# A scan layer on one Trainium2 core: the work that prepares the next block is put at other steps

## The chip, the core and the metric

The kernel runs on one core of one Trainium2 chip. The metric is the device time of one execution in microseconds (us), lower is better. Before the change it is 2182.27 us, the median of 3 runs (2181.54 to 2183.92). One more execution was recorded by the profiler: its own time is 2181.55 us, and its span, from the first to the last instruction, 2179.8 us.

## The reference

The program is a decoder of six stages. Only the first is touched, a selective state-space (Mamba) layer over 2 sequences of 1024 rows with 256 features. `hidden_states` is the normalised input; its result is added to the input.

```python
D_MODEL, D_STATE, D_CONV = 256, 16, 4
D_INNER, DT_RANK = 512, 16
x, z = split(hidden_states @ in_proj_w.T)
x = silu(causal_conv(x, conv_w, 4 taps) + conv_b)
A = -exp(A_log)
dt, Bm, C = split(x @ x_proj_w.T)              # 16, 16, 16 columns
dt = softplus(dt @ dt_proj_w.T + dt_proj_b)
def step(h, ins):                              # over the 1024 rows
    h = exp(dt_t[:, :, None] * A) * h + dt_t[:, :, None] * B_t[:, None, :] * x_t[:, :, None]
    y = einsum('bdn,bn->bd', h, C_t)
y = ys + x * D
return y * silu(z) @ out_proj_w.T
```

## The kernel before

The 2048 rows are cut into NK = 4 **blocks** of W = 512 rows; blocks 1 and 2 are the first sequence, 3 and 4 the second (the code counts them k = 0 to 3). The 512 inner channels are CI = 4 groups of 128, and there are NS = 16 states. A block is NU = 64 **steps** p = 0 to 63, one for each state and channel group: step p has state p // 4 and group p % 4, on a tile of 128 channels by 512 rows. One step passes through all engines:

- ScalarE multiplies dt·x by B in a layout with the rows in partitions, one quarter of a state's tile per step (`times_b`, into `UT`), and makes the decay exp(dt·A) (`decay`, into `dA`).
- TensorE turns the product into the layout with channels in partitions (`bring_u`, into one of two PSUM banks).
- VectorE runs the recurrence over 512 rows in one instruction (`scan`, into a ring `H` of 8 tiles).
- GpSimd multiplies two steps' states by C in one instruction, after the even and the odd step are both scanned (`times_c`, into a ring `HC` of 8).
- TensorE turns `HC` back and sums it over the states in PSUM banks 0 to 3 (`sum_up`), LAG = 5 steps later.

Each engine takes its instructions strictly in the order of the program, and engines wait on each other by semaphores. `bring_u` of step G waits until scan G-2 has ended; `decay` of step G until scan G-6 has; the first `times_b` of a state until the `bring_u` of the state before it has ended; `sum_up` until `times_c` has. So the order in which each engine's list is written out decides what a wait holds up.

Besides the 64 steps each block carries the **preparation** of the block after it and the end of the block before it, written out by tables of step numbers in the five engines' loops. On the preparation's path lie: the projection of x (`project_x`), the convolution of 4 instructions for each group on VectorE (`convolve`), silu (`silu_x`), the projections to B, C and dt (`project_rows`, `transpose_b`, `project_dt`), softplus in pieces on ScalarE, VectorE and GpSimd (`magnitude`, `rectify`, `correct`, `logarithm`, `add_logarithm`), the product with x (`times_x`) and its transpose (`transpose_dtx`, `keep_dtx`). The end of a block is the gate with silu(z) on VectorE (`gate`), transposes of the gated tile (`transpose_gated`, `keep_gated`), the output projection (`project_out`) and the addition to the rows (`add_rows`). Silu and logarithm each need another function table on ScalarE than exp, so that a table load stands before and after them.

PSUM banks 6 and 7 are shared by all of the preparation; `bank(i, ...)` makes TensorE wait until the last user of the bank has been read.

Of the kernel before, what the change touches and what calls it, by code (L numbers as in the profile page):

```python
# [6 lines left out]
ALU = mybir.AluOpType  # L7
# [7 lines left out]
P = 128  # L15
# [208 lines left out]
G_ORDER = (0, 2, 1, 3)  # L224


def mamba(g, a):
    nc = g.nc
    PS = g.PS
    with ExitStack() as ctx:  # L230
# [53 lines left out]
        with nc.Block() as block:  # L284
# [24 lines left out]
            def _(pe):  # L309
# [64 lines left out]
                def transpose_dtx(k, c):  # L374

                    out = bank(c % 2, dtxt_ready, k * CI + c + 1)
# [12 lines left out]
                def transpose_gated(k, i):  # L389

                    t = G_ORDER[i]
                    out = bank(t % 2, g_ready, k * TC + i + 1)
# [5 lines left out]
                def project_out(k, t, half):  # L398

                    if half == 0:  # L400
                        if t % 2 == 0:
                            held[t // 2] = bank(t // 2, o_used, k * 2 + t // 2 + 1)
                        pe.wait_ge(g_ready, (k + 1) * TC)
                    out = held[t // 2][:, t % 2 * D:(t % 2 + 1) * D]
# [16 lines left out]
                def sum_up(G):  # L421
# [3 lines left out]
                    if u == 0 and k:  # L425
                        pe.wait_ge(y_used, k * TC)
                    pe.wait_ge(hc_ready, G + 1)
                    for t in range(TC):
                        ins = pe.matmul(PS[t][:, c * P:(c + 1) * P], HC[:, G % YR, t * P:(t + 1) * P], g.ident[:, :],  # L429
                                        start=(u == 0), stop=(u == NU - 1), is_transpose=True, skip_group_check=True)  # L430
# [17 lines left out]
                for k in range(NK):  # L448
                    for p in range(NU):
# [3 lines left out]
                        if 8 <= p < 11:  # L453
                            sum_up(k * NU + 2 * (p - 8))
                            sum_up(k * NU + 2 * (p - 8) + 1)
                        elif p >= 11:
                            sum_up(k * NU + p - LAG)
                        if k + 1 < NK:
# [4 lines left out]
                            if p in (10, 11, 14, 15):  # L463
                                project_x(k + 1, 2 + (p - 10) // 4, p % 2)
                        if k and p in (8, 9, 12, 13):
                            transpose_gated(k - 1, (8, 9, 12, 13).index(p))
                        if p in (12, 13, 18, 19):
                            if p == 12 and k == 0:
                                pe.wait_ge(diag_ready, 1)
                            add_skip(k, (12, 13, 18, 19).index(p))  # L470
                        if p in (16, 17, 20, 21):
                            project_z(k, (p - 16) // 4, p % 2)
                        if k + 1 < NK:
                            if 23 <= p < 27:
                                project_rows(k + 1, p - 23)
                            if p == 27:
                                transpose_b(k + 1)
                            if 28 <= p < 32:
                                project_dt(k + 1, p - 28)
                        if k and 32 <= p < 40:  # L480
                            project_out(k - 1, (p - 32) // 2, p % 2)
                        if 40 <= p < 44:
                            project_z(k, 2 + (p - 40) // 2, p % 2)
                        if k + 1 < NK and p in (46, 50, 54, 58):
                            transpose_dtx(k + 1, (p - 46) // 4)
# [9 lines left out]
            def _(act):  # L495
# [53 lines left out]
                def keep_dtx(k, c):  # L549

                    act.wait_ge(dtxt_full, k * CI + c + 1)
                    act.activation(DTXT[:, k % 2, :, c * P:(c + 1) * P], PS[6 + c % 2][:, :].rearrange("p (t n) -> p t n", t=TC),
                                   ACT.Copy).then_inc(dtxt_ready, 1)

                def keep_gated(k, i):

                    t = G_ORDER[i]
                    act.wait_ge(g_full, k * TC + i + 1)
# [49 lines left out]
                for k in range(NK):  # L608
                    for p in range(NU):
# [6 lines left out]
                        if k and p in (9, 10, 13, 14):  # L616
                            keep_gated(k - 1, (9, 10, 13, 14).index(p))
                        if p == 20:
# [2149 lines left out]
```

## Time and profile before

| what | value |
|---|---|
| median of 3 runs | 2182.27 us (2181.54 to 2183.92) |
| the profiled execution: time, span | 2181.55 us, 2179.8 us |
| first scan starts, last scan ends | 57.0 us, 613.9 us |
| block 1, 2, 3, 4, first scan to the next block's first scan (block 4: to its last scan's end) | 151.0, 152.1, 152.8, 101.1 us |
| busy from 57 to 614 us: PE, DVE, ACT, POOL | 421.1, 368.7, 396.7, 380.3 us of 557 |
| mean granted TensorE clock from 57 to 614 us | 0.87 |

The scan layer is the first 634 us of the span; the five stages behind it are the same code in both kernels. No engine is busy for more than four fifths of the layer. Block 4 has no next block to prepare and takes 50 us less than each of the others.

### The profile page before, as it was taken

How to read it: one execution, taken by the hardware profiler on the slowest of the kernel's cores; microseconds unless marked ns; L12 is line 12 of the kernel's file. 1: busy time of each engine (PE TensorE's matmuls, PEld its weight loads, DVE VectorE, ACT ScalarE, POOL GpSimd, SP SyncE). 2: the span in 40 equal slices, each digit the busy share in tenths (PEclk: the TensorE clock that was granted, in tenths of full speed). 3: DMA queues.
4: the chain of work that ended last, by engine and by line, in shares of the span. 5: the costliest groups of instructions: out<-in, count | busy, mean ns of one | idle time of the engine just before them, and what ended most of it. 6: DMA issues, size and time to landing. Idle time of an engine off the chain costs nothing. (4 is left out here: it accounts for less than half of the span.)

```text
span 2179.8 us, 28324 instructions
## 1 busy us (share of the span) xinstructions
PE 1572.5 (72%) x9844; PEld 1325.8 (61%) x9844; DVE 1119.2 (51%) x2193; ACT 912.1 (42%) x1599; POOL 930.2 (43%) x615
## 2 busy tenths in 40 slices
PE   4776866857868974863038996898692199989990
PEld 1555655657656863861027895895592088878880
DVE  6755756746767951225766345645847023222322
ACT  4775776767834442532124223744331022322220
POOL 0577576577643334651023112402005723685406
PEclk7988988988979976985558998899895599999995
DMA  3001010101011032520010001002005311333103
GB/s 110 20 21 39 20 40 20 40 20 40 20 63 28 1 117 98 187 75 23 0 47 1 1 1 42 1 11 69 1 1 210 104 63 49 126 114 109 30 20 118
DMA packets 51958, 114.44 MB, mean 53 GB/s; under 512 B 13996, under 2 KB 34377, under 8 KB 44276
## 3 DMA queue, kind: packets, MB, share of 16 engines
q1 hardware_dynamic: 43764, 75.23, 10.0%
q0 software_dynamic: 8064, 37.45, 5.1%
q8 instruction: 85, 1.39, 0.3%
q14 instruction: 45, 0.37, 0.1%
HBM read 87.02 MB, written 25.87 MB: 52 GB/s over the span
## 5 line engine op out<-in xcount | busy, mean ns | idle before, releaser
L839 POOL TENSOR_TENSOR HC<-H,CB 128x1024 f32<-128x1024 f32 x128 | 302.5, 2364 | 165.7 <-DVE H L739 103.7
L418 PE MATMUL ps<-ident,UT 128*128 128x128 f32 x1024 | 182.1, 307 | 58.5 <-DVE H L739 52.4
L739 DVE TENSOR_TENSOR_SCAN H<-dA,ps 128x512 f32<-128x512 f32 x128 | 154.0, 1214 | 124.6 <-PE ps L418 86.2
L418 PEld LDWEIGHTS ps<-ident,UT 128*128 128x128 f32 x1024 | 136.7, 158 | 131.0 <-DVE H L739 72.0
L570 ACT ACTIVATE UT<-DTXT,BT 128x512 f32<-128x512 f32 x256 | 181.4, 711 | 39.3 <-PE ps L418 39.2
L739 DVE TENSOR_TENSOR_SCAN H<-dA,HL,ps 128x512 f32<-128x512 f32 x128 | 160.2, 1275 | 71.7 <-PE ps L418 46.0
L580 ACT ACTIVATE dA<-DT,nA 128x512 f32<-128x512 f32 x256 | 180.8, 709 | 2.8 <-DVE DT L707 2.7
L429 PE MATMUL ps<-ident,HC 128*128 128x128 f32 x1024 | 171.5, 298 | 9.7 <-POOL HC L839 9.2
L1748 POOL TENSOR_TENSOR f_W<-f_stage,f_zeros 128x2048 fp32r<-128x2048 f32 x24 | 86.5, 3606 | 144.6 <-POOLq L1768 138.6
L429 PEld LDWEIGHTS ps<-ident,HC 128*128 128x128 f32 x1024 | 138.1, 157 | 12.5 <-POOL HC L839 10.9
L1965 DVE TENSOR_TENSOR f_XN<-f_XN,ps 128x1024 f32<-128x1024 f32 x39 | 47.6, 1221 | 173.5 <-PE ps L147 173.5
L145 PE MATMUL ps<-f_W,f_DIT 128*128 x312 | 128.7, 412 | 8.8 <-POOL f_W L1750 7.1
L146 PE MATMUL ps<-f_W,f_DIT 128*128 x312 | 125.0, 401 | 0.0
L147 PE MATMUL ps<-f_W,f_DIT 128*128 x312 | 124.9, 400 | 0.0
L1750 POOL TENSOR_TENSOR f_W<-f_stage,f_W 128x2048 fp32r<-128x2048 f32 x24 | 110.3, 4595 | 1.9
L1958 DVE TENSOR_TENSOR f_HT<-ps,f_HT 128x512 fp32r<-128x512 f32 x78 | 50.2, 686 | 100.9 <-ACT f_HT L1862 100.9
L1519 POOL TENSOR_TENSOR f_l<-f_w,f_h 128x2048 fp32r<-128x2048 f32 x16 | 73.5, 4596 | 64.2 <-ACT f_h L1580 63.5
L138 PE MATMUL ps<-ident,h_XN 128*128 128x128 f32 x96 | 29.4, 432 | 84.7 <-DVE h_XN L96 59.3
L1873 ACT ACTIVATE f_EO<-ps 128x256 f32<-128x256 f32 x39 | 14.9, 383 | 179.6 <-PE ps L147 179.6
L145 PE MATMUL ps<-f_W,f_HT 128*128 x312 | 87.8, 281 | 1.8 <-issue 1.8
L146 PE MATMUL ps<-f_W,f_HT 128*128 x312 | 87.9, 282 | 0.0
L147 PE MATMUL ps<-f_W,f_HT 128*128 x312 | 87.8, 282 | 0.0
(490 smaller groups left out, 4306.7 us busy)
## 6 DMA issues: line engine op xcount, KB each, us to landing
f_stage<-in_f_w POOLq DMA_DIRECT2D x24, 1024.0 KB, 5.4
CB<-m_c_rows SPq DMA_DIRECT2D x16, 1024.0 KB, 4.7
f_w<-in_f_w SPq DMA_DIRECT2D x16, 1024.0 KB
f_rows_in<-f_zeros SPq DMA_DIRECT2D x13, 384.0 KB, 13.6
f_DI<-f_rows_in SPq DMA_DIRECT2D x39, 128.0 KB, 2.2
f_rows_out<-f_EO SPq DMA_DIRECT2D x39, 128.0 KB, 1.7
a_values<-a_zeros SPq DMA_DIRECT2D x8, 320.0 KB, 5.4
a_VBD<-a_values SPq DMA_DIRECT2D x8, 320.0 KB, 4.5
```

The costliest lines, as they stand in the source:

```text
L145: pe.matmul(out, ah, bh, start=first, stop=False)
L146: pe.matmul(out, ah, bl, start=False, stop=False)
L147: return pe.matmul(out, al, bh, start=False, stop=last)
L418: ins = pe.transpose(PS[4 + G % UR][:, t * P:(t + 1) * P], UT[:, n % 2, t, c * P:(c + 1) * P], g.ident[:, :])
L429: ins = pe.matmul(PS[t][:, c * P:(c + 1) * P], HC[:, G % YR, t * P:(t + 1) * P], g.ident[:, :], start=(u == 0), stop=(u == NU - 1), is_tra ...
L570: act.activation(UT[:, N % 2, t, :], DTXT[:, k % 2, t, :], ACT.Copy, scale=BT[:, k % 2, t, n:n + 1]).then_inc(ut_ready, 1)
L580: act.activation(dA[:, G % AR, :], DT[:, k % 2, c, :], ACT.Exp, scale=nA[:, c, n:n + 1]).then_inc(da_ready, 1)
L739: dve.tensor_tensor_scan(H[:, G % HR, :], dA[:, G % AR, :], PS[4 + G % UR][:, :], first, ALU.mult, ALU.add).then_inc(h_ready, 1)
L839: pool.tensor_tensor(HC[:, y:y + 2, :], H[:, s:s + 2, :], CB[:, n // 4 % CR, n % 4:n % 4 + 1, :].to_broadcast([P, 2, W]), ALU.mult).then_i ...
L1519: pool.tensor_tensor(l[:, e % 2, :, :], w[:, e % WR, :, :], h[:, e % 2, :, :].bitcast(F32), ALU.subtract).then_inc(wl_ready, 1)
L1748: pool.tensor_tensor(hi, stage[:, q, :], zeros[:, 0:1].to_broadcast([P, PART]), ALU.add).then_inc(hi_ready, 1)
L1750: pool.tensor_tensor(lo, stage[:, q, :], hi.bitcast(F32), ALU.subtract).then_inc(lo_ready, 1)
```

## The change

It keeps every computation of the layer and moves the preparation to other steps, in the lists of all five engines. The new positions (before in brackets): x projection of groups 2 and 3 at steps 7, 8, 10, 11 (10, 11, 14, 15); two convolution instructions a step at steps 4, 5, 7, 8, 9, 10, 12, 13 (one a step at 4 to 19); silu of x after step 14 (20); projections to B, C and dt at steps 15 to 24 (23 to 31); magnitude and rectify at 21, 22, 24, 25 (29 to 32); correct at 24, 27, 30, 33 (30, 32, 34, 36); the logarithms after step 37, behind the first two silus of z (40, and silus of z at 20); add_logarithm at 39, 43, 47, 51 (42, 46, 50, 54) and times_x at 41, 45, 49, 53 (44, 48, 52, 56) on GpSimd; transpose_dtx at 47, 51, 55, 59 (46, 50, 54, 58) on TensorE. The z projections stand at 32 to 35 and 38 to 41 (16, 17, 20, 21 and 40 to 43), the gated transposes at 26, 27, 29, 30 (8, 9, 12, 13) and the output projection at 44 to 54 (32 to 39), with add_rows at 48 and 55 (36 and 40).

Three things are more than a new place. The product with D, which was added into the sums at steps 12 to 19, now opens them at steps 6 to 9 (`begin_sums`) and waits there for the gate of the same rows; the sums over states start at step 10 instead of 8, three at step 10 and two at 11 to 13. All four transposes of dt·x use bank 6 alone, where they alternated between two. The output projection uses bank 7 alone. The product with C is over two steps in both kernels; only a loop over single steps is put around it, so that other work can stand behind an odd step.

```diff
-                    out = bank(c % 2, dtxt_ready, k * CI + c + 1)
+                    out = bank(0, dtxt_ready, k * CI + c + 1)
...
-                def add_skip(k, t):
-
+                def begin_sums(k, t):
+
+                    if k:
+                        pe.wait_ge(y_used, (k - 1) * TC + t + 1)
                     for c in range(CI):
                         ins = pe.matmul(PS[t][:, c * P:(c + 1) * P], XS[:, c, t * P:(t + 1) * P], skip_diag[:, c, :],
-                                        start=False, stop=False, skip_group_check=True)
+                                        start=(c == 0), stop=False, skip_group_check=True)
...
-                            held[t // 2] = bank(t // 2, o_used, k * 2 + t // 2 + 1)
+                            held[1] = bank(1, o_used, k * 2 + t // 2 + 1)
...
-                        if 8 <= p < 11:
-                            sum_up(k * NU + 2 * (p - 8))
-                            sum_up(k * NU + 2 * (p - 8) + 1)
-                        elif p >= 11:
+                        if p == 10:
+                            sum_up(k * NU)
+                        if 10 <= p < 14:
+                            sum_up(k * NU + 2 * p - 19)
+                            sum_up(k * NU + 2 * p - 18)
+                        elif p >= 14:
                             sum_up(k * NU + p - LAG)
...
-                        if k + 1 < NK and p in (46, 50, 54, 58):
-                            transpose_dtx(k + 1, (p - 46) // 4)
+                        if k + 1 < NK and p in (47, 51, 55, 59):
+                            transpose_dtx(k + 1, (p - 47) // 4)
...
-                            if 42 <= p < 58 and p % 4 == 2:
-                                add_logarithm(k + 1, (p - 42) // 4)
-                            if 44 <= p < 60 and p % 4 == 0:
-                                times_x(k + 1, (p - 44) // 4)
+                            if p in (39, 43, 47, 51):
+                                add_logarithm(k + 1, (p - 39) // 4)
+                            if p in (41, 45, 49, 53):
+                                times_x(k + 1, (p - 41) // 4)
```

TensorE in block 2, before, around the first transpose of dt·x (L379 of `DTX`, step 46); L418 is bring_u, L429 sum_up, L347 the z projection of step 43:

```order
L347 MATMUL ps<-w_in,XT 128x512
L418 MATMUL ps<-ident,UT 128x128 x4
L429 MATMUL ps<-ident,HC 128x128 x4
L418 MATMUL ps<-ident,UT 128x128 x4
L429 MATMUL ps<-ident,HC 128x128 x4
L418 MATMUL ps<-ident,UT 128x128 x4
L429 MATMUL ps<-ident,HC 128x128 x4
L379 MATMUL ps<-ident,DTX 128x128 x4
```

The same place in the changed kernel (step 47; bring_u is L418, sum_up L427, the output projection L406, the transpose L378):

```order
L406 MATMUL ps<-m_w_out,GD 128x256 x2
L418 MATMUL ps<-ident,UT 128x128 x4
L427 MATMUL ps<-ident,HC 128x128 x4
L406 MATMUL ps<-m_w_out,GD 128x256 x2
L418 MATMUL ps<-ident,UT 128x128 x4
L427 MATMUL ps<-ident,HC 128x128 x4
L378 MATMUL ps<-ident,DTX 128x128 x4
L418 MATMUL ps<-ident,UT 128x128 x4
L427 MATMUL ps<-ident,HC 128x128 x4
L406 MATMUL ps<-m_w_out,GD 128x256 x2
```

The transpose stands one step later, and the output projection is now among these steps. The sum_up in front of it is that of step 41 before and of step 42 now.

ScalarE in block 2, before, behind step 40: the logarithms (L547), then times_b (L570) and decay (L580) of step 41:

```order
L547 ACT_TABLE_LOAD
L547 ACTIVATE EA<-EA 128x512 x4
L570 ACTIVATE UT<-DTXT,BT 128x512
L580 ACT_TABLE_LOAD
L580 ACTIVATE dA<-DT,nA 128x512
```

And in the changed kernel, behind step 37 (silu of z L523, logarithm L550, times_b L572, decay L582):

```order
L523 ACT_TABLE_LOAD
L523 ACTIVATE ZT<-ps 128x512 x2
L550 ACT_TABLE_LOAD
L550 ACTIVATE EA<-EA 128x512 x4
L572 ACTIVATE UT<-DTXT,BT 128x512
L582 ACT_TABLE_LOAD
L582 ACTIVATE dA<-DT,nA 128x512
```

The first two silus of z, which stood behind silu_x at step 20, are now in front of the logarithms, with a table load of their own.

GpSimd in block 2, before, at the corrections (L808 to L810, three instructions for a channel group); L839 is times_c:

```order
L839 TENSOR_TENSOR HC<-H,CB 128x1024 x17
L808 TENSOR_SCALAR DTX<-EA 128x512
L809 TENSOR_SCALAR DTX<-DTX 128x512
L810 TENSOR_TENSOR DTX<-EA,DTX 128x512
L839 TENSOR_TENSOR HC<-H,CB 128x1024
```

And in the changed kernel, from the corrections of the first group (L812 to L814) to times_c and the second group's:

```order
L843 TENSOR_TENSOR HC<-H,CB 128x1024 x14
L812 TENSOR_SCALAR DTX<-EA 128x512
L813 TENSOR_SCALAR DTX<-DTX 128x512
L814 TENSOR_TENSOR DTX<-EA,DTX 128x512
L843 TENSOR_TENSOR HC<-H,CB 128x1024
```

The first count includes the last product of block 1, so that 16 products of block 2 stood ahead of the first correction and 13 stand there now.

## Rows read from the trace of the kernel before

**Rows 1.** Busy time by block (stretch, then PE, PEld, DVE, ACT, POOL, clock, DMA).
```profile
57.00:208.00 151.00, 107.71 (x610) 82.78 (x609) 92.93 (x90) 101.88 (x160) 101.08 (x76) 0.84 0.06 22
208.00:360.00 152.00, 113.85 (x669) 89.69 (x668) 98.85 (x99) 105.63 (x167) 100.29 (x58) 0.87 0.08 29
360.00:513.00 153.00, 113.56 (x666) 89.83 (x666) 94.50 (x93) 104.15 (x164) 103.19 (x77) 0.85 0.07 28
513.00:614.00 101.00, 85.94 (x604) 72.73 (x602) 82.44 (x70) 84.99 (x134) 75.73 (x34) 0.95 0.09 32
```

**Rows 2.** Who waited for whom, blocks 2 and 3 (us in total, times, longest).
```profile
DVE H L739 <- PE ps L418: 76.2, 52, 7.0
...
PE ps L379 <- POOL DTX L824: 45.9, 8, 6.3
...
DVE H L739 <- ACT dA L580: 33.1, 12, 7.2
```

**Rows 3.** Busy time, block 2: steps 0 to 20, and steps 41 to 58.
```profile
208.00:248.50 40.50, 36.84 (x236) 28.91 (x235) 38.68 (x46) 28.55 (x46) 25.42 (x12) 0.92 0.15 53
...
298.30:348.00 49.70, 26.64 (x142) 24.18 (x142) 22.45 (x18) 27.80 (x43) 35.36 (x21) 0.73 0.06 21
```

**Rows 4.** GpSimd in order of time, block 2 (start, duration, instruction, idle before it).
```profile
315.93 2.37 POOL L839 TENSOR_TENSOR HC<-H,CB 128x1024 f32<-128x1024 f32 x1 [3.63 <-issue]
318.25 1.29 POOL L818 TENSOR_TENSOR DTX<-DTX,EA 128x512 f32<-128x512 f32 x1
...
320.84 2.34 POOL L839 TENSOR_TENSOR HC<-H,CB 128x1024 f32<-128x1024 f32 x1
323.13 1.26 POOL L824 TENSOR_TENSOR DTX<-DT,XS 128x512 f32<-128x512 f32 x1
328.03 2.38 POOL L839 TENSOR_TENSOR HC<-H,CB 128x1024 f32<-128x1024 f32 x1 [3.63 <-issue]
```

**Rows 5.** TensorE in order of time, block 2, the second transpose of dt·x.
```profile
324.54 1.08 PE L379 MATMUL ps<-ident,DTX 128*128 128x128 f32 x4 [5.30 <-POOL DTX L824]
```

**Rows 6.** VectorE in order of time, block 2: steps 26 and 27, 31 and 32, 51.
```profile
263.49 1.28 DVE L739 TENSOR_TENSOR_SCAN H<-dA,HL,ps 128x512 f32<-128x512 f32 x1 [0.73 <-PE ps L418]
265.51 1.28 DVE L739 TENSOR_TENSOR_SCAN H<-dA,HL,ps 128x512 f32<-128x512 f32 x1 [0.73 <-PE ps L418]
...
273.32 1.28 DVE L739 TENSOR_TENSOR_SCAN H<-dA,HL,ps 128x512 f32<-128x512 f32 x1 [0.43 <-ACT dA L580]
...
275.69 1.28 DVE L739 TENSOR_TENSOR_SCAN H<-dA,HL,ps 128x512 f32<-128x512 f32 x1 [0.50 <-ACT dA L580]
...
326.61 1.28 DVE L739 TENSOR_TENSOR_SCAN H<-dA,HL,ps 128x512 f32<-128x512 f32 x1 [6.24 <-PE ps L418]
```

**Rows 7.** GpSimd, block 2: the products on either side of one correction.
```profile
279.73 2.38 POOL L839 TENSOR_TENSOR HC<-H,CB 128x1024 f32<-128x1024 f32 x1
...
284.72 2.38 POOL L839 TENSOR_TENSOR HC<-H,CB 128x1024 f32<-128x1024 f32 x1
```

**Rows 8.** ScalarE, block 2: the silus behind step 20.
```profile
246.43 1.28 ACT L515 ACT_TABLE_LOAD   x1
247.72 2.19 ACT L515 ACTIVATE XS<-DT 128x512 f32<-128x512 f32 x4
249.82 1.09 ACT L520 ACTIVATE ZT<-ps 128x512 f32<-128x512 f32 x2
```

**Rows 9.** ScalarE, block 2: the last logarithm, behind step 40.
```profile
294.78 0.63 ACT L547 ACTIVATE EA<-EA 128x512 f32<-128x512 f32 x1 [3.18 <-POOL DTX L810]
```

**Rows 10.** VectorE, block 2: steps 60 and 61, and the first scan of block 3.
```profile
352.43 1.28 DVE L739 TENSOR_TENSOR_SCAN H<-dA,HL,ps 128x512 f32<-128x512 f32 x1 [0.35 <-PE ps L418]
353.62 1.12 DVE L663 TENSOR_SCALAR m_XN<-X,m_mv,m_rstd 128x256 f32<-128x256 f32 x1
354.67 1.27 DVE L739 TENSOR_TENSOR_SCAN H<-dA,HL,ps 128x512 f32<-128x512 f32 x1
...
360.03 1.21 DVE L739 TENSOR_TENSOR_SCAN H<-dA,ps 128x512 f32<-128x512 f32 x1
```

More of the change, by code:

```diff
@@ L429, in sum_up @@
                         ins = pe.matmul(PS[t][:, c * P:(c + 1) * P], HC[:, G % YR, t * P:(t + 1) * P], g.ident[:, :],
[L430 removed]
+                                        start=False, stop=(u == NU - 1), is_transpose=True, skip_group_check=True)
                     ins.then_inc(hc_used, 1)
@@ L462, in _ @@
                                 project_x(k + 1, (p - 2) // 2, p % 2)
[L463 to L468, printed above, removed]
+                            if p in (7, 8):
+                                project_x(k + 1, 2, p - 7)
@@ L477, in _ @@
                                 transpose_b(k + 1)
[L478 to L483, printed above, removed]
-                        if k + 1 < NK and p in (46, 50, 54, 58):
-                            transpose_dtx(k + 1, (p - 46) // 4)
+                            if p in (20, 21, 23, 24):
+                                project_dt(k + 1, (20, 21, 23, 24).index(p))
@@ new lines, in _ @@
+                        if k and p in (26, 27, 29, 30):
+                            transpose_gated(k - 1, (26, 27, 29, 30).index(p))
+                        if 32 <= p < 36:
+                            project_z(k, (p - 32) // 2, p % 2)
+                        if 38 <= p < 42:
+                            project_z(k, 2 + (p - 38) // 2, p % 2)
+                        if k + 1 < NK and p in (47, 51, 55, 59):
+                            transpose_dtx(k + 1, (p - 47) // 4)
+                        if k and p in (44, 45, 46, 48, 50, 52, 53, 54):
+                            i = (44, 45, 46, 48, 50, 52, 53, 54).index(p)
+                            project_out(k - 1, i // 2, i % 2)
@@ L721, in add_rows @@
                     rows = g.X[:, k * TC + 2 * j:k * TC + 2 * j + 2, :]
-                    dve.tensor_tensor(rows, rows, PS[6 + j][:, :].rearrange("p (t d) -> p t d", t=2), ALU.add).then_inc(o_used, 1)
+                    dve.tensor_tensor(rows, rows, PS[7][:, :].rearrange("p (t d) -> p t d", t=2), ALU.add).then_inc(o_used, 1)
                 def scan(G):
@@ L848, in _ @@
                 for k in range(NK):
-                    for p in range(0, NU, 2):
-                        times_c(k * NU + p)
+                    for p in range(NU):
+                        if p % 2 == 0:
+                            times_c(k * NU + p)
                         if k + 1 < NK:
-                            if p == 2 and (k + 1) % KB:
+                            if p == 3 and (k + 1) % KB:
                                 edges(k + 1)
-                            if 30 <= p < 38:
-                                correct(k + 1, (p - 30) // 2)
-                            if 42 <= p < 58 and p % 4 == 2:
-                                add_logarithm(k + 1, (p - 42) // 4)
-                            if 44 <= p < 60 and p % 4 == 0:
-                                times_x(k + 1, (p - 44) // 4)
+                            if p in (24, 27, 30, 33):
+                                correct(k + 1, (p - 24) // 3)
+                            if p in (39, 43, 47, 51):
+                                add_logarithm(k + 1, (p - 39) // 4)
+                            if p in (41, 45, 49, 53):
+                                times_x(k + 1, (p - 41) // 4)
 NH, HD, SK = 16, 16, 77
```

83 lines of the change are left out of this document (41 added, 42 removed).

## The prediction

> **What bounds the kernel now.** I read the busy time by block first. Blocks 1 to 3 take 151, 152 and 153 us for 64 steps, block 4 takes 101, and no engine fills any of them: the fullest, ScalarE, is busy 105.63 of 152 us in block 2, GpSimd 100.29 and VectorE 98.85 [rows 1]. So the layer is bound by waits in blocks 1 to 3, and their shortest possible length is set by the fullest engine, not by 152. The rest of the program, from 634 us on, is untouched by the change.
>
> The view of who waited for whom says which waits. In blocks 2 and 3 the scan waited 76.2 us for TensorE and 33.1 us for the decay [rows 2]. TensorE was no bound itself: it waited 45.9 us, eight times, in front of the transpose of dt·x for GpSimd's product with x [rows 2], and bring_u stood behind it. The order of time shows one such turn. From GpSimd's times_c at 315.93 to the next turn's at 328.03 are 12.10 us, of which it works without a gap from 315.93 to 323.13 + 1.26 = 324.39, that is 8.46 us, and then idles 3.63 us [rows 4]. TensorE starts its transpose at 324.54, as soon as the product is there, after 5.30 us idle [rows 5], and the scan that comes behind it starts at 326.61 after 6.24 us idle [rows 6]. It is a closed chain: scan, times_c, times_x, transpose, bring_u, scan. Between steps 41 and 58 GpSimd is busy 35.36 of 49.7 us and TensorE, at a mean clock of 0.73, 26.64 [rows 3].
>
> The scan's waits for the decay are table loads on ScalarE: behind step 20 a load of 1.28 us and six silus of 2.19 + 1.09 us [rows 8], behind step 40 four logarithms, of which the last waited 3.18 us for GpSimd's correction [rows 9].
>
> **The change at the transposes (steps 38 to 59).** The two kernels' lists on GpSimd are alike here, three steps earlier, and TensorE's transposes stand one step later. The lead grows from 2 steps to 6. More than that, the wait can't come back: at step 47 + 4c TensorE first does the sum of step 42 + 4c, which needs times_c of that pair, and GpSimd has times_x(c) in front of that times_c. Whoever waits for the sum has waited for the product with x already. What is late next is GpSimd's own work, 8.46 us for four steps against 12.10.
>
> **GpSimd as the bound (steps 24 to 55).** The corrections move from steps 30 to 36 up to 24 to 33, and add_logarithm to 39. So from times_c of step 24 to that of step 54 GpSimd holds 16 products with C and all of its extra work. Four turns at 8.46 us hold eight of the products; four products with a correction take 284.72 - 279.73 = 4.99 us each [rows 7]; four more are bare at 2.37 us [rows 4]. Sum: 33.8 + 20.0 + 9.5 = 63.3 us. The scan alone would need about 1.2 us a step (354.67 less the 1.12 us of L663 less 352.43, and the mutual overlap of some 0.1) [rows 10], 37 us for 31 steps; ScalarE and TensorE have less extra work there than GpSimd. A lag of some five steps is allowed (the sum of step p - 5 stands behind bring_u of step p), which the end of this stretch uses up.
>
> The logarithms, behind step 37, do cost a wait for the decay: three loads of 1.28, two silus of 1.09, four logarithms of some 0.6 each, then an ordinary step of 1.2, in all 8.6 us, against two scans that are still supplied (2.4): some 6 us without a scan. By my reckoning GpSimd works through them, since it then stands behind by two plain products and two with a correction (2 x 2.37 + 2 x 4.99 = 14.7 us), so that they add nothing. If it had no such lag they would add the 6 us; this is the second rival. The last logarithm finds its correction ready, three steps of distance in place of four but without the extra products behind it.
>
> Behind the stretch: the sum and the last transpose, 0.5 and 0.9 us, the copy 0.6, and one ScalarE step of 1.2 until scan 60, because the first times_b of the new block needs all four transposed groups; then steps 60 to 63 as before, 360.03 - 352.43 = 7.6 us [rows 10]. Sum 10.8.
>
> **The front of the block.** Steps 0 to 13 now hold what VectorE had in 0 to 19: all sixteen convolution instructions and the gates. In the old stretch of 21 scans it was busy 38.68 of 40.5 us [rows 3]; seven scans fewer are 38.68 - 8.4 = 30.3 busy, and with the same small gaps 31.7 us. TensorE has room: it was busy 36.84 us at a clock of 0.92 for 21 steps, and the z projections and gated transposes leave. The opening of the sums waits for gates that VectorE does at steps 5 and 6, a step before TensorE needs them; I take nothing for it (0 to 1.5 us a block).
>
> Step 14: the last silu can start only when step 13's convolution ends. Then 0.55 (a quarter of 2.19) + 1.28 for the load back + 1.2 for the ordinary pair = 3.0 us until the next scan. In blocks 1 and 3 all four silus wait for the edge of the convolution: 1.6 more. Steps 15 to 23 carry the projections to B, C and dt as 23 to 31 did: between 2.02 us (265.51 - 263.49) and 2.37 us (275.69 - 273.32) where there is a projection [rows 6], less at the two steps without; 9 x 2.0 = 18.0 us. Steps 24 and 25, until GpSimd starts the long stretch: 3.6.
>
> **Sum for block 2:** 31.7 + 3.0 + 18.0 + 3.6 + 63.3 + 10.8 = 130.4 us against 152: 21.6 less. Blocks 1 and 3 move the same work, with 1.6 us more at step 14 and somewhat less elsewhere (no gates in block 1, no normalisation at the end of block 3): 21 each. Block 4 has no preparation; its silus, z and output projections are only placed elsewhere: 0 (bounds -5 and +3, the waits at its two table episodes). At the end of the layer the second half of the output projection waits for add_rows in bank 7, about +1 us, and the gated transposes no longer share a bank two by two, about -1. In all -63 to -64.
>
> The places at which no row can show a wait (triple sums at step 10, the gates, four copies of dt·x through a single bank, ScalarE reaching step 59 before TensorE) I put at 1.2 us a block, bounds 0 and 6 us. That makes **-60 us**: 2181.55 - 60 = 2121.6 for the profiled execution, whose own time is 0.7 us under the median, so 2122.
>
> **A rule on table loads.** Each of blocks 1 to 3 has seven loads instead of six. The rows: the load at 246.43 takes 1.28 us, and the silu starts at 247.72, right behind it [rows 8]. The Trainium skill (ScalarE: Activation LUTs, section What ACT_TABLE_LOAD costs) gives about 1.28 us for the load and about 1.38 us for a drain with it, 2.66 us for every switch. By that rule the three added loads would be an estimated 8 us of ScalarE's time instead of 3.8. The trace has no such drain between the two rows, so the sum stays with 1.28.
>
> **Rivals.**
> 1. *GpSimd isn't behind when ScalarE loads tables.* Then the 6 us behind step 37 stand in the sum by themselves, and only what the transposes and the front give is left: 3 x 6 = 18 us back, 2140. For it: at step 40 before, the scan was held by the same kind of work. Against it: GpSimd has 20 us of corrections and products in ten steps there. Chance 0.22.
> 2. *VectorE's normalisation waits for GpSimd.* At step 60 it takes 1.12 us for 256 columns [rows 10], more than half a scan. If GpSimd never rests at a block's end, all four in blocks 1 and 2 meet a product in flight, with up to 2.37 us and 1.2 in the mean to wait; a little over 3 us more for each of the two blocks, 2128. The Trainium skill (SBUF — State Buffer, section SBUF: two separate sides) says that GpSimd and such a VectorE operation take a shared port exclusively, for a whole instruction. Chance 0.08.
> 3. *The waits go and the time stays,* because ScalarE or TensorE take GpSimd's place for the whole of it. Against it: ScalarE is busy 105.63 of 152 us, TensorE 113.85 [rows 1]; either would have to keep 40 us of idle time. Chance 0.03, 2180.
> 4. *Slower: TensorE at its lower level where its work is crowded.* Steps 0 to 23 now hold the x projections, the opening of the sums, triple sums and all the projections to B, C and dt in a row. If the 1.2 GHz level held there, the 26 us of work that I count in steps 0 to 13 (36.84 less the work of seven plain steps and the projections that leave) would be 52 against 31.7, and steps 15 to 23 would take 35 instead of 18: +37 a block, +111 in all against the 60 saved. It decides from a little over half of these steps at the lower level; at three quarters the time is 2205. Against it: the granted clock was 0.92 in the old front [rows 3] and 0.95 in block 4, the block with the fewest idle times [rows 1]; it was low, 0.73, where TensorE waited. Chance 0.05.
>
> **Numbers.** The forecast, 2122, has 0.62. A measurement of this kernel can tell 0.2%, some 4 us, from no change. Faster by more than that are the forecast and rivals 1 and 2: 0.92; within 0.2% 0.03, slower 0.05. Range: from 2102 (no hidden waits, -5 in block 4, and the projection steps nearer to 1.5 us) to 2150 (rival 1 with 3 us a block of hidden waits).
>
> **What would show it.** Right: the waits of the transpose (L378) for times_x near nothing; blocks 1 to 3 at 128 to 134 us; GpSimd busy for over nine tenths from times_c 24 to 54, through the episode behind step 37; a mean clock of TensorE above 0.87; block 4 within 5 us of 101. Wrong: a GpSimd idle time of 5 us behind step 37 (rival 1), normalisations of 2 us (rival 2), ScalarE waiting at the copies of dt·x, or steps 0 to 13 longer than 36 us.

## The result, and the profile after

The changed kernel takes 2118.54 us, the median of 4 runs (2118.11 to 2121.53), against 2183.1 us, the median of 4 runs of the kernel before taken with it. The ratio is 0.9705, 95% interval 0.9688 to 0.9722: 3.0% faster, 64.6 us. The forecast was 2122.

Busy time by block in the changed kernel (columns as in [rows 1]; the blocks begin at their first scans at 59.6, 194.1, 325.9 and 458.6 us):

```profile
59.60:194.00 134.40, 104.03 (x609) 77.54 (x607) 92.79 (x89) 102.17 (x161) 100.62 (x76) 0.88 0.07 24
194.10:326.00 131.90, 105.24 (x670) 80.10 (x670) 99.02 (x100) 105.99 (x168) 100.25 (x58) 0.96 0.09 33
326.00:458.50 132.50, 103.62 (x664) 77.04 (x662) 94.44 (x92) 103.68 (x165) 102.84 (x76) 0.97 0.09 33
458.50:552.30 93.80, 82.68 (x605) 68.54 (x604) 82.04 (x71) 84.72 (x134) 75.80 (x34) 1.00 0.10 35
```

The four blocks are 134.5, 131.8, 132.6 and 93.7 us long, against 151.0, 152.1, 152.8 and 101.1 [rows 1]: 16.5, 20.3, 20.2 and 7.4 less. The work of VectorE, ScalarE and GpSimd in them is the same to 1 us; what went is idle time. TensorE has the same matmuls and is busy 9 and 10 us less in blocks 2 and 3, at a mean granted clock of 0.96 and 0.97 against 0.87 and 0.85. The first scan starts 2.7 us later than before, and what stands behind the last scan takes 1.7 us less. Together -63.3 us of span.

The transpose of dt·x waited 45.9 us for GpSimd in blocks 2 and 3 [rows 2]. In all of the trace its waits for GpSimd are gone; what is left is this (the view of the line L378, the former L379):

```profile
its engine sat idle before it (us, times) until:
  ACT DTXT L555: 17.4, 6
  issue: 7.5, 1
  DVE DTX L711: 6.0, 1
```

TensorE still waits for GpSimd in these two blocks, but at another place and for less: in front of the sums (L427), for the product with C. Before, the same wait (then L429) was 2.6 us, in two places.

```profile
PE ps L427 <- POOL HC L843: 24.1, 16, 2.5
```

GpSimd in order of time shows one turn of four steps, which answers to [rows 4]:

```profile
295.52 2.34 POOL L843 TENSOR_TENSOR HC<-H,CB 128x1024 f32<-128x1024 f32 x1
297.83 1.28 POOL L822 TENSOR_TENSOR DTX<-DTX,EA 128x512 f32<-128x512 f32 x1
299.19 1.28 POOL L823 TENSOR_TENSOR DT<-DT,DTX 128x512 f32<-128x512 f32 x1
300.43 2.36 POOL L843 TENSOR_TENSOR HC<-H,CB 128x1024 f32<-128x1024 f32 x1
302.75 1.27 POOL L828 TENSOR_TENSOR DTX<-DT,XS 128x512 f32<-128x512 f32 x1
303.98 2.36 POOL L843 TENSOR_TENSOR HC<-H,CB 128x1024 f32<-128x1024 f32 x1
```

The turn takes 303.98 - 295.52 = 8.46 us, without any idle time, where it was 12.10. From the product of step 24 to the end of that of step 54 GpSimd takes 66.3 us (248.50 to 314.8), 63.1 of them work. It is idle once, for 3.17 us behind the product that answers to step 36, while ScalarE loads its tables (first fence: GpSimd, second: ScalarE, third: VectorE, all of block 2):

```profile
265.77 2.37 POOL L843 TENSOR_TENSOR HC<-H,CB 128x1024 f32<-128x1024 f32 x1
268.10 0.62 POOL L812 TENSOR_SCALAR DTX<-EA 128x512 f32<-128x512 f32 x1
268.80 0.62 POOL L813 TENSOR_SCALAR DTX<-DTX 128x512 f32<-128x512 f32 x1
269.51 1.27 POOL L814 TENSOR_TENSOR DTX<-EA,DTX 128x512 f32<-128x512 f32 x1
270.74 4.66 POOL L843 TENSOR_TENSOR HC<-H,CB 128x1024 f32<-128x1024 f32 x2
278.57 2.37 POOL L843 TENSOR_TENSOR HC<-H,CB 128x1024 f32<-128x1024 f32 x1 [3.17 <-issue]
```

```profile
267.20 1.28 ACT L523 ACT_TABLE_LOAD   x1
268.49 1.09 ACT L523 ACTIVATE ZT<-ps 128x512 f32<-128x512 f32 x2
269.60 1.28 ACT L550 ACT_TABLE_LOAD   x1
270.89 2.19 ACT L550 ACTIVATE EA<-EA 128x512 f32<-128x512 f32 x4
272.99 0.71 ACT L572 ACTIVATE UT<-DTXT,BT 128x512 f32<-128x512 f32 x1
273.71 1.28 ACT L582 ACT_TABLE_LOAD   x1
275.00 0.72 ACT L582 ACTIVATE dA<-DT,nA 128x512 f32<-128x512 f32 x1
```

```profile
275.93 3.73 DVE L741 TENSOR_TENSOR_SCAN H<-dA,HL,ps 128x512 f32<-128x512 f32 x3 [6.66 <-ACT dA L582]
```

The logarithms no longer wait for the correction (four in one row, where the last waited 3.18 us [rows 9]), but the scan still stands for 6.66 us.

Two more waits matter below. At the end of block 2, TensorE waits in front of the sum of step 54, and then ScalarE for the last transpose. Before, ScalarE waited at each of the block's four copies of dt·x (22.7 us together, 6.2 us at the last); only this one is left:

```profile
314.84 1.11 PE L427 MATMUL ps<-ident,HC 128*128 128x128 f32 x4 [1.05 <-POOL HC L843]
315.75 1.06 PE L378 MATMUL ps<-ident,DTX 128*128 128x128 f32 x4
```

```profile
316.85 0.60 ACT L555 ACTIVATE DTXT<-ps 128x512 f32<-128x512 f32 x1 [4.77 <-PE ps L378]
```

The transpose of the last group stands behind the sum of step 54, and that waits for GpSimd. Ahead of block 1, the transposes in their one bank take turns with the copies, two of them waiting 0.69 us for the copy before:

```profile
50.34 1.12 PE L378 MATMUL ps<-ident,DTX 128*128 128x128 f32 x4 [6.72 <-ACT DTXT L555]
52.14 1.11 PE L378 MATMUL ps<-ident,DTX 128*128 128x128 f32 x4 [0.69 <-ACT DTXT L555]
53.94 1.11 PE L378 MATMUL ps<-ident,DTX 128*128 128x128 f32 x4 [0.69 <-ACT DTXT L555]
```

### The profile page after: what moved, and what is told of

Its sections match the earlier page's. It is cut to its first block and busy times, and to the rows that moved or that the text cites. A ratio compares the mean times of both kernels' runs of the same rounds, so it can differ in the third digit from the quotient of the medians.

```text
span 2116.5 us, 28324 instructions
## 1 busy us (share of the span) xinstructions
PE 1546.2 (73%) x9844; PEld 1292.9 (61%) x9844; DVE 1119.3 (53%) x2193; ACT 912.7 (43%) x1602; POOL 930.2 (44%) x615
## 5 line engine op out<-in xcount | busy, mean ns | idle before, releaser
L572 ACT ACTIVATE UT<-DTXT,BT 128x512 f32<-128x512 f32 x256 | 181.3, 711 | 55.7 <-PE ps L418 55.3
L418 PE MATMUL ps<-ident,UT 128*128 128x128 f32 x1024 | 167.2, 288 | 50.2 <-DVE H L741 40.7
L418 PEld LDWEIGHTS ps<-ident,UT 128*128 128x128 f32 x1024 | 122.2, 146 | 123.9 <-DVE H L741 61.8
L427 PE MATMUL ps<-ident,HC 128*128 128x128 f32 x1024 | 159.0, 284 | 37.2 <-POOL HC L843 37.1
L582 ACT ACTIVATE dA<-DT,nA 128x512 f32<-128x512 f32 x256 | 181.0, 709 | 2.8 <-DVE DT L709 2.7
L427 PEld LDWEIGHTS ps<-ident,HC 128*128 128x128 f32 x1024 | 124.0, 147 | 45.0 <-POOL HC L843 44.8
```

The costliest lines, as they stand in the source:

```text
L418: ins = pe.transpose(PS[4 + G % UR][:, t * P:(t + 1) * P], UT[:, n % 2, t, c * P:(c + 1) * P], g.ident[:, :])
L572: act.activation(UT[:, N % 2, t, :], DTXT[:, k % 2, t, :], ACT.Copy, scale=BT[:, k % 2, t, n:n + 1]).then_inc(ut_ready, 1)
L582: act.activation(dA[:, G % AR, :], DT[:, k % 2, c, :], ACT.Exp, scale=nA[:, c, n:n + 1]).then_inc(da_ready, 1)
```

## The experiments

Twelve kernels, each timed against the kernel before. Ratios are to the kernel before on the same chip, with the 95% interval. The rows come from three chips, the first four from one, the next four and the last four from two others, on which the kernel before took 2183.5, 2185.1 and 2182.7 us; so medians of different groups are comparable to some 2 us only. The lengths are from each kernel's profiled execution; a step's length is the time from its scan's start to the next scan's. Two profiled executions of the same changed kernel differ by up to 2 us in a block (132.6 and 134.7 in block 3), so that a block's length alone tells only larger differences.

```
kernel                          median us  ratio (interval)          first scan  blocks 1 to 4 (us)         last scan ends
changed, again                  2119.5     0.9713 (0.9693 to 0.9733)  59.8       132.5 130.9 134.7  93.7    551.7
lead undone                     2177.1     0.9974 (0.9961 to 0.9986)  60.3       150.5 151.4 154.2  94.8    611.3
late part alone                 2130.9     0.9756 (0.9734 to 0.9778)  56.9       132.8 135.9 138.0 103.0    566.7
one addition less               2093.2     0.9599 (0.9576 to 0.9621)  59.7       128.1 126.4 128.0  93.7    535.9
no silu table at step 37        2103.1     0.9628 (0.9612 to 0.9644)  59.9       131.1 129.5 132.8  91.9    545.3
one subtraction less            2114.8     0.9677 (0.9660 to 0.9693)  60.3       130.7 129.3 131.4  94.8    546.5
two banks ahead of block 1      2118.2     0.9696 (0.9680 to 0.9713)  57.6       132.5 131.0 134.5  93.7    549.3
last transpose at step 58       2116.0     0.9686 (0.9670 to 0.9702)  59.9       132.5 130.7 132.3  93.6    549.0
same, normalisation at step 14  2110.8     0.9666 (0.9651 to 0.9680)  59.7       129.9 128.9 133.5  93.6    545.6
silu table early                2116.7     0.9697 (0.9682 to 0.9712)  59.8       132.7 130.9 131.5  93.7    548.6
copy of z, silu later           2114.1     0.9684 (0.9669 to 0.9699)  59.8       132.9 129.7 131.3  93.0    546.7
all of the last five            2101.3     0.9623 (0.9610 to 0.9637)  56.9       127.9 127.1 131.7  91.9    535.5
```

**The changed kernel again.**

> The changed kernel once more, as the measure for the others of this series on the same chip. Every theory: 2118 to 2121 us, blocks 134, 132, 132 and 94 us.

It came as expected, and it is the measure for the lengths below.

**The lead undone.**

```diff
-                            if p in (41, 45, 49, 53):
-                                times_x(k + 1, (p - 41) // 4)
+                            if p in (44, 48, 52, 56):
+                                times_x(k + 1, (p - 44) // 4)
```

(add_logarithm back at 42, 46, 50, 54, the transposes at 46, 50, 54, 58; ScalarE's copies of them stay at the changed kernel's steps)

> The changed kernel, but add_logarithm at 42, 46, 50, 54, times_x at 44, 48, 52, 56 and the transposes of dt·x at 46, 50, 54, 58, as before the change. Theory A (the lead of GpSimd's product with x over its transpose is the largest part of the gain): the closed chain is back, a turn of four steps takes 12.1 us in place of 8.5, three to four turns a block: about +10 us a block, +30 in all, some 2149 us, and TensorE waits 40 to 70 us in front of the transposes again. Rival B (the gain came from the front of the block and from the order of the table loads; the turns are held by ScalarE or TensorE anyway): less than +8 us, under 2127.

Blocks 1 to 3 are 18, 20.5 and 19.5 us longer than in the changed kernel, 58 us in all: A holds, B is out, and A's price was half of the real one. TensorE waits 66.1 us in twelve places for times_x. GpSimd in order of time shows the turn:

```profile
315.06 2.38 POOL L843 TENSOR_TENSOR HC<-H,CB 128x1024 f32<-128x1024 f32 x1 [5.11 <-issue]
317.40 1.28 POOL L822 TENSOR_TENSOR DTX<-DTX,EA 128x512 f32<-128x512 f32 x1
...
319.97 2.34 POOL L843 TENSOR_TENSOR HC<-H,CB 128x1024 f32<-128x1024 f32 x1
322.27 1.26 POOL L828 TENSOR_TENSOR DTX<-DT,XS 128x512 f32<-128x512 f32 x1
328.68 2.37 POOL L843 TENSOR_TENSOR HC<-H,CB 128x1024 f32<-128x1024 f32 x1 [5.14 <-issue]
```

It is 13.62 us long, not the 12.10 of [rows 4], with the same 8.5 us of work. The difference is the output projections, which the change put among these steps and which now stand on the closed chain as well: block 1 has none, and its three turns take 12.12, 12.09 and 12.13 us.

**The late part alone, in the kernel before.**

```diff
-                    for p in range(0, NU, 2):
-                        times_c(k * NU + p)
+                    for p in range(NU):
+                        if p % 2 == 0:
+                            times_c(k * NU + p)
...
-                            if 44 <= p < 60 and p % 4 == 0:
-                                times_x(k + 1, (p - 44) // 4)
+                            if p in (41, 45, 49, 53):
+                                times_x(k + 1, (p - 41) // 4)
```

(add_logarithm, the transposes and their copies at the changed kernel's steps too)

> The kernel before with this part of the change alone: add_logarithm at 39, 43, 47, 51, times_x at 41, 45, 49, 53, transposes of dt·x at 47, 51, 55, 59 (still in two banks), their copies at 49, 53, 57, 59. Theory A: 10 to 13 us less a block, 2145 to 2153 us. Rival B: 2170 to 2180. The wait behind step 40 (9 us, where the last logarithm waits for the correction) should stay under both, since nothing ahead of it moves.

18.2, 16.2 and 14.8 us less in blocks 1 to 3, 53 us less in the median (2130.9), more than A said. The wait behind step 40 stayed, 9.01 us from scan 40 to scan 41, as expected. So the lead by itself is worth three quarters of the whole gain in the layer (47.2 of 62.2 us at its last scan), and the rest of the reordering, on top of it, 15 us of the layer's end (566.7 to 551.7): 0.3, 5.0, 3.3 and 9.2 us in the four blocks, less the 2.9 us by which the first scan is late. These lengths are from an execution of 2136.55 us, the longest of four (2127.03 to 2136.55); by the medians the lead alone is worth 53 of 64 us, and the rest on top of it 11. How block 2 is divided, from the starts of its scans:

```
                    steps 0 to 45   steps 46 to 63
before                  100.6            51.5
changed                  95.4            36.4
lead undone              95.4            56.0
late part alone         102.6            33.4
```

In this block the lead acts in steps 46 to 63 alone, and what the other moves give stands in steps 0 to 45.

**One addition less on GpSimd.**

```diff
-                    sums(pool.tensor_tensor(DTX[:, c, :], DTX[:, c, :], EA[:, c, :], ALU.add))
-                    pool.tensor_tensor(o, o, DTX[:, c, :], ALU.add).then_inc(dt_ready, 1)
+                    pool.tensor_tensor(DTX[:, c, :], DTX[:, c, :], EA[:, c, :], ALU.add).then_inc(dt_ready, 1)
```

> The changed kernel without the second addition of add_logarithm (the relu part is not added, so dt is the relu part alone): one GpSimd instruction of 1.28 us less for each channel group, 5.1 us a block in steps 39 to 51. Theory A (GpSimd is the bound from step 38 to 54): -5.1 a block, -12 to -15 in all, 2104 to 2107. Rival C (TensorE with the output projections, or ScalarE, would hold the same pace): 0 to -4 us.

The last scan ends 15.8 us earlier, 15.4 was the full price of twelve instructions. In each of blocks 1 to 3, steps 38 to 53 alone are 3.1 to 3.3 us shorter: GpSimd is the bound from step 38 to 54, and C is out. The median fell by 26 us, and what stands behind the layer, with another input, took 11 us less, 1554.9 against 1566.0 us (why is open); for this kernel and the next the layer is to be compared and not the total.

**No silu table at step 37.**

```diff
-                    act.activation(ZT[:, t, :], PS[6 + t % 2][:, :], ACT.Silu).then_inc(z_ready, 1)
+                    act.activation(ZT[:, t, :], PS[6 + t % 2][:, :], ACT.Copy if t < 2 else ACT.Silu).then_inc(z_ready, 1)
```

> The changed kernel with a plain copy in place of the silu for the first two tiles of z, so that ScalarE's episode behind step 37 loads one table less in blocks 1 to 3 and none (of two) in block 4; the gate is wrong for these rows. Forecast (GpSimd works through the episode and is the bound): nothing in blocks 1 to 3, about -2.6 us in block 4. Rival 1 of the prediction (ScalarE's episode is on the path by itself; GpSimd idles behind it, 3.2 us in block 2 of the trace): -1.3 a block as well, together -6 to -7 us.

The layer ends 6.4 us earlier: the number given for rival 1, 1.4 to 1.9 us a block. The step of the episode fell from 7.91 to 6.48 us in block 2 and GpSimd's idle time behind it from 3.17 to 1.71 us. So the episode is on the path, even though GpSimd had work for most of it.

**One subtraction less on GpSimd, ahead of the episode.**

```diff
-                    sums(pool.tensor_scalar(DTX[:, c, :], DTX[:, c, :], 1.0, -1.0, ALU.mult, ALU.add))
-                    pool.tensor_tensor(DTX[:, c, :], EA[:, c, :], DTX[:, c, :], ALU.subtract).then_inc(corr_ready, 1)
+                    pool.tensor_scalar(DTX[:, c, :], DTX[:, c, :], 1.0, -1.0, ALU.mult, ALU.add).then_inc(corr_ready, 1)
```

> The changed kernel without the last subtraction of correct (exp(-|x|) less its rounded value, so the correction is not formed): one GpSimd instruction of 1.29 us less for each group, 5.2 us a block in steps 24 to 33, ahead of the logarithms. If GpSimd is the bound from step 24 on through the episode: -12 to -15 us. If the episode behind step 37 lets GpSimd catch up (it idles 3.2 us there in block 2 already): only what TensorE and the scan wait for before step 37, so -1 to -7 us, with GpSimd's idle time behind step 37 grown from 3 to 5 or 7 us.

The last scan ends 5.2 us earlier, a third of the 15.5 us taken out, and GpSimd's idle time behind step 37 doubled (this kernel's GpSimd, the first product after the episode, where the changed kernel has 3.17):

```profile
273.84 2.36 POOL L842 TENSOR_TENSOR HC<-H,CB 128x1024 f32<-128x1024 f32 x1 [6.21 <-issue]
```

So the stretch from step 24 to 54 is two stretches with a wait for ScalarE between them. In the first, two thirds of the price did not come back, so other engines hold the block there too; in this kernel's block 2 most of the scans between 249 and 260 us that wait at all wait for ScalarE's decay, 0.4 us each. Which of the others it is was not separated. Only the second stretch is GpSimd's alone.

**Two banks ahead of block 1.**

```diff
-                    out = bank(0, dtxt_ready, k * CI + c + 1)
+                    out = bank(0 if k else c % 2, dtxt_ready, k * CI + c + 1)
```

(and the copy reads the same bank)

> The changed kernel with the four transposes of dt·x ahead of block 1 in banks 6 and 7 in turn, as before the change; in the blocks bank 6 alone as changed. In the trace the first scan starts at 59.6 us and not at 57.0, with each of these transposes behind the copy of the one before. If the single bank is the cause: -2.6 us, 2116; otherwise 0.

The first scan starts at 57.64 us, 2.2 us earlier than in the changed kernel run again, of the 2.8 us by which that one is later than the kernel before: the single bank is the cause of most of it. (The last kernel of the table has the two banks too, and starts at 56.9.) The medians, 2118.2 and 2119.5, don't tell the two kernels apart by themselves.

**The last transpose at step 58.**

```diff
-                        if k + 1 < NK and p in (47, 51, 55, 59):
-                            transpose_dtx(k + 1, (p - 47) // 4)
+                        if k + 1 < NK and p in (47, 51, 55, 58):
+                            transpose_dtx(k + 1, (47, 51, 55, 58).index(p))
```

> The changed kernel with the last transpose of dt·x at step 58 in place of 59, ahead of the sum of step 54. In the trace ScalarE waits 4.8 us at step 59 for that transpose, which stands behind times_c of step 54 at TensorE, though its own data have been there for 2.3 us; scan 60 starts 5.1 us after scan 59. If this order is the cause: 2 to 3 us less at each of three blocks' ends, -6 to -9 in all, 2110 to 2113. If GpSimd's pace would hold scan 60 anyway: 0 to -2.

A miss: the layer ends 2.7 us earlier, not 6 to 9, and nearly all of that is in block 3, whose steps 59 and 60 take 3.5 us together where they took 5.9. That is the 2 to 3 us expected for each block. Block 3 is the one that has no normalisation at its end. In block 2 step 59 fell from 4.46 to 2.24 us and step 60 rose from 1.50 to 3.45. VectorE (first fence) and GpSimd (second) of this kernel show why:

```profile
314.31 1.28 DVE L741 TENSOR_TENSOR_SCAN H<-dA,HL,ps 128x512 f32<-128x512 f32 x1 [0.96 <-PE ps L418]
315.51 2.33 DVE L665 TENSOR_SCALAR m_XN<-X,m_mv,m_rstd 128x256 f32<-128x256 f32 x1
317.76 1.27 DVE L741 TENSOR_TENSOR_SCAN H<-dA,HL,ps 128x512 f32<-128x512 f32 x1
318.95 0.38 DVE L665 TENSOR_SCALAR m_XN<-X,m_mv,m_rstd 128x256 f32<-128x256 f32 x1
```

```profile
310.67 7.01 POOL L843 TENSOR_TENSOR HC<-H,CB 128x1024 f32<-128x1024 f32 x3
319.16 2.39 POOL L843 TENSOR_TENSOR HC<-H,CB 128x1024 f32<-128x1024 f32 x1 [1.47 <-DVE H L741]
```

The normalisation takes 2.33 us when GpSimd's products run until 317.68, and 0.38 us when GpSimd is idle as it starts. The mechanism of rival 2, which had cost little in the changed kernel since its scan 60 came so late, took the place of the wait removed. With the rule that the prediction cites there from the Trainium skill (SBUF — State Buffer, section SBUF: two separate sides) the trace agrees: the first normalisation ends 0.16 us after the GpSimd product in flight.

**The same, with the normalisations behind step 14.**

```diff
-                        if k + 2 < NK and p >= NU - TC:
-                            normalize(k + 2, p - NU + TC)
+                        if k + 2 < NK and p == 14:
+                            for t in range(TC):
+                                normalize(k + 2, t)
```

> The changed kernel with the last transpose of dt·x at step 58 and, besides, the four normalisations for the block after the next behind step 14 instead of one behind each of steps 60 to 63. With the transpose alone moved, step 59 fell from 4.5 to 2.2 us in block 2, and step 60 rose from 1.5 to 3.5, with a normalisation of 2.33 us that ends 0.16 us after a run of three GpSimd products. Theory D (the normalisation waits for GpSimd's product in flight): behind step 14 VectorE idles for a table load, so nothing is lost there, and steps 59 to 63 take 1.2 to 2 us each: blocks 1 and 2 end at 127 to 129 us, 2 to 4 less each than with the transpose alone, 2109 to 2112 in all. Rival E (step 60 is held by GpSimd's pace or by the first scan inputs of the new block, the normalisation only fills the gap): no more than 1 us a block.

2110.8 us, and the last scan ends 3.4 us earlier than with the transpose alone. Behind step 14 all four normalisations take 1.36 us together, in time that VectorE waits for ScalarE's table, and steps 60 to 63 of block 2 take 1.23, 1.23, 1.22 and 1.20 us. Block 1 is 2.6 and block 2 1.8 us shorter, at and just under the lower end of D. Block 2 would have gained 3 us, but its steps 1 and 2 are 0.5 to 0.6 us longer each, and so are block 3's: part of the time comes back at the start of the next block, for a reason that no run here separates. E (no more than 1 us a block) is out.

**The silu table early.**

```diff
                             if p == 14:
+                                act.activation(warm[:, 0:1], g.eps[:, 0:1], ACT.Silu)
                                 for c in range(CI):
                                     silu_x(k + 1, c)
```

> The changed kernel with one silu of a single column on ScalarE in front of the silus behind step 14, before their wait, so that the silu table is loaded while ScalarE waits for the edge. In blocks 1 and 3 the trace has the load of 1.28 us start only after the edge was added, and step 15 there takes 6.5 us. If that load is on the path: 1.3 us less in each of blocks 1 and 3, -2.6 us in all; block 2 (load already hidden) unchanged.

The step in question, from scan 14 to scan 15 (step 14 as counted here, 15 in the expectation), takes 5.22 us in blocks 1 and 3 instead of 6.50, exactly the load, and block 2's is unchanged at 3.65. Two loads make 2.6 us; the 3.1 by which the layer ends earlier holds some noise. ScalarE of the changed kernel in block 3, with the load behind the wait for the edge:

```profile
358.03 1.28 ACT L518 ACT_TABLE_LOAD   x1 [6.90 <-DVE DT L690]
359.32 2.19 ACT L518 ACTIVATE XS<-DT 128x512 f32<-128x512 f32 x4
```

**Copy of z behind step 37, its silu behind step 43.**

```diff
+                    if t == 2:
+                        act.wait_ge(z_ready, k * TC + 2)
+                        for u in range(2):
+                            act.activation(ZT[:, u, :], ZT[:, u, :], ACT.Silu)
                     act.wait_ge(z_full, k * TC + t + 1)
-                    act.activation(ZT[:, t, :], PS[6 + t % 2][:, :], ACT.Silu).then_inc(z_ready, 1)
+                    act.activation(ZT[:, t, :], PS[6 + t % 2][:, :], ACT.Copy if t < 2 else ACT.Silu).then_inc(z_ready, 1)
```

> The changed kernel with a plain copy of the first two tiles of z out of PSUM behind step 37, and their silu in place behind step 43, in front of the silus of the other two; the result is the same as the reference. One table load less a block (two at step 37 in block 4). With the silus left out altogether the layer got 6.5 us shorter. If ScalarE has a lead at step 43 in blocks 1 to 3, the two silus there are hidden: -4 to -6 us. If not, each costs 0.55 us: -2 us.

The layer ends 5.0 us earlier: step 37 is 6.47 instead of 7.91 us in block 2, step 43 5.11 instead of 4.31. Steps 38 to 53 of block 2 take 29.0 us in both kernels, so that this added 0.8 us is hidden behind GpSimd's pace. As expected.

**All of the last five together.**

> The changed kernel with all of these: the transposes ahead of block 1 in two banks, the last transpose at 58, normalisations behind step 14, the silu table loaded early, z copied behind step 37 and its silu behind 43. Result as the reference. If the parts add (-2.2, -6 to -8, -2.6, -4 to -6): 2100 to 2105 us. If GpSimd's pace eats half of them: about 2110.

2101.3 us (5 runs, 2099.4 to 2103.5), 81 us or 3.8% faster than the kernel before, its interval clear of the changed kernel's. The layer's last scan ends 16.2 us earlier than in the changed kernel; the single parts, two banks 2.4, transpose and normalisation 6.1, table 3.1, copy of z 5.0, make 16.6. They add, as far as lengths that differ by up to 2 us a block between executions can tell.

## Why the prediction was right

The forecast of -60 us was measured as -64.6. Term by term, for block 2:

```
term                                               forecast   measured
steps 0 to 13                                        31.7       31.7
step 14                                               3.0        3.7
steps 15 to 23                                       18.0       15.2
until the product of step 24                          3.6        3.8
GpSimd, product of step 24 to the end of 54          63.3       66.3
from there to scan 60                                 3.2        4.3
steps 60 to 63                                        7.6        6.9
sum                                                 130.4      131.8
```

- *The transposes.* Right: the wait went and could not come back, since the sum in front of the transpose needs a later product than the transpose does. Undoing that lead took back 58 of 64 us (medians). What is left of TensorE's waits for GpSimd, 24.1 us in front of the sums in blocks 2 and 3, is the pace of GpSimd's own work.
- *GpSimd as the bound.* Right in its work (63.1 us measured, 63.3 worked out from [rows 4] and [rows 7]) and wrong in one step: "GpSimd works through them ... so that they add nothing". The 14.7 us of work by which it was to stand behind were not there. When ScalarE starts its first load, at 267.20, GpSimd is in the product of step 32; that, the last correction and the products of steps 34 and 36 end at 275.40, 8.2 us later. The program does not let GpSimd fall as far behind as I put it: bring_u of step 37 stands behind the sum of step 31, so the product of step 30 is done by then. And I left out that the next product needs two more scans, 38 and 39, the first of which starts at 275.93: it starts at 278.57, after 3.17 us idle. With 14.7 us of work from 267.20 on, GpSimd would by this count have been busy until 281.9 and not have idled. The idle time is half of rival 1's 6 us: rival 1 holds as a mechanism (the table and the subtraction experiments), at half of its price. And ahead of step 37 GpSimd was not the only bound, as only a third of what was taken from it there came back.
- *The front.* Steps 0 to 13 to the tenth. Steps 15 to 23 were put too long: steps 15 and 16 take only 1.22 each, as TensorE has done their projections (225.53 and 228.35) before scan 15 starts at 229.51, and steps 17, 19 and 23 take 1.7, 1.4 and 1.2.
- *Step 14 in blocks 1 and 3.* Steps 13 and 14 take 10.1 us there against 6.3 in block 2, 3.8 more; I had put 1.6, for the three silus that lose their cover. Missing were the table load of 1.28 us, which stands behind ScalarE's wait for the edge and is not hidden (the experiment with the early table took just this off), and the addition of the edge itself, 0.98 us on VectorE in step 13.
- *Block 4.* -7.4 us, outside the bounds of -5 and +3 that I gave to 0. Its z projections and gated transposes made the old front steps 1.7 us long; in the new places many of them fall into the two waits for ScalarE, which are there anyway, and these are shorter too (the steps that hold them take 4.8 and 4.3 us, where they took 6.4 and 4.7). This is read from the steps' lengths; no run tests it.
- *Ahead of block 1.* The first scan is 2.7 us later, most of it for the single bank; I looked for the bank's price only inside the blocks, at steps 47 to 59, where TensorE's transposes wait for no copy.
- *Rule on table loads.* The three loads of one episode are each followed within 0.02 us by their function, at 268.49, 270.89 and 275.00. The drain that the Trainium skill (ScalarE: Activation LUTs, section What ACT_TABLE_LOAD costs) adds does not show here either. One load less on the path was worth 1.28 us (table early) and 1.43 us (step 37 of block 2 without the silu table).
- *Rival 4* (the lower clock level) went the other way: the granted clock rose from 0.87 and 0.85 to 0.96 and 0.97 in blocks 2 and 3.
- *The signs.* Of what was to show a wrong forecast, one came: ScalarE waits at a copy of dt·x, the last of each block (4.77 us in block 2), and scan 60 comes 1.1 us later than I put it. Block 1, at 134.5 us (132.5 in the second execution), and block 4, at 93.7, are outside the lengths that were to show it right.

That the total came out within 4 us of the forecast owes something to chance: the misses of +3.0 and +1.1 us at GpSimd and ScalarE in block 2, +2.2 in each of blocks 1 and 3, and +2.7 ahead of block 1 met -2.8 in steps 15 to 23 and -7.4 in block 4. Block 1 gave 16.5 us (18.4 in the second execution) where 21 was forecast.

## What to carry to other kernels

Where engines take turns in a ring, a producer that is only one turn ahead of its consumer closes a chain through all of them; compare the producer's place with the wait in front of the consumer, and if what is waited for there already implies the producer, the chain is open for good. The same move has another price in another order: by the medians the lead was worth 58 us on top of the rest and 53 alone, the rest 11 on top of the lead and 6 without it (by the layer's last scan 60 and 47, 15 and 3). When a wait is removed, look at what the next engine does in the time that comes free: here a 0.4 us normalisation became 2.3 us.

## What the runs showed of the hardware

A VectorE subtraction and product over 256 columns in and out of SBUF takes 0.38 us when GpSimd is idle as it starts and up to 2.33 us when it meets a GpSimd product in flight; it then ends 0.1 to 0.2 us after the product. The scan in front of it, which reads one input from PSUM, takes its usual 1.28 us beside the same product. And a table load is issued with the function that needs it, behind that function's wait: one silu of a single column ahead of the wait took 1.28 us off the path.
